# A causal transformer block with routed low-rank experts: its PSUM banks divided anew, and its side work dealt out one piece a step

## What is computed

```python
h = layernorm(x) * (1 + ca) + sa
q, k, v = split(h @ W_qkv.T + b_qkv)            # 16 heads of 16
o = softmax(causal(q @ k.T / 4)) @ v
x = x + ga * (o @ W_out.T + b_out)
h = layernorm(x) * (1 + cb) + sb
h1 = relu(mole(h; W1, b1, A1, B1, R1))          # 256 -> 1024
x = x + gb * mole(h1; W2, b2, A2, B2, R2)       # 1024 -> 256
# mole(x) = x @ W + b + (1/8) * sum_e softmax(x @ R)_e * (x @ A_e) @ B_e,   3 experts of rank 8
```

## Time and profile before

| | |
|---|---|
| median of 3 runs | 1724.15 us (1717.27 to 1735.03) |
| the profiled execution: its time, its span | 1730.61 us, 1728.9 us |
| busy: PE, PEld | 1412.8 us (82%), 796.4 us (46%) |
| busy: DVE, ACT, POOL | 961.8 us (56%), 685.5 us (40%), 561.6 us (32%) |
| mean granted clock of TensorE | 0.808 |

### The profile page before, as it was taken

How to read it: one execution, slowest core, us unless ns; L and a number is a source line. 1 busy time by engine, 2 the same in 40 slices (tenths; PEclk the granted TensorE clock), 3 DMA queues, 4 the chain that set the end, 5 groups by cost and what they waited for, 6 DMA issues and landing times. The chain is left out here.

```text
span 1728.9 us, 26273 instructions
## 1 busy us (share of the span) xinstructions
PE 1412.8 (82%) x10096; PEld 796.4 (46%) x10096; DVE 961.8 (56%) x1878; ACT 685.5 (40%) x935; POOL 561.6 (32%) x680
## 2 busy tenths in 40 slices
PE   4458898897998989899857988889888889899445
PEld 4334454544544434454423554536453445454245
DVE  6146566566576676763336556665756667761212
ACT  1113354353443445355522433344533444546210
POOL 5460151324440124332302341234432233233262
PEclk8666588788996888888965786888995899899758
DMA  5242223121321121220241223113121112100000
GB/s 149 77 133 79 74 81 101 34 64 31 99 71 49 38 55 57 67 77 20 80 114 47 75 87 83 34 37 104 51 75 40 48 30 71 50 10 13 31 18 13
DMA packets 83638, 106.68 MB, mean 62 GB/s; under 512 B 9002, under 2 KB 57074, under 8 KB 83516
## 3 DMA queue, kind: packets, MB, share of 16 engines
q1 hardware_dynamic: 83516, 105.01, 21.5%
HBM read 66.71 MB, written 37.75 MB: 60 GB/s over the span
## 5 line engine op out<-in xcount | busy, mean ns | idle before, releaser
L853 DVE TENSOR_REDUCE mx<-ps 128x1 f32<-128x512 f32 (+3 forms) x1152 | 706.8, 655 | 436.7 <-PE ps L570 241.0
L759 ACT ACTIVATE prob<-ps 128x1024 f32<-128x1024 f32 (+3 forms) x640 | 567.1, 896 | 700.1 <-PE ps L548 368.6
L570 PE MATMUL ps<-kst,qst 48*128 48x512 f32 (+3 forms) x1280 | 321.7, 497 | 135.5 <-DVE mx L853 108.5
L607 PE MATMUL ps<-prob,vw 128*17 128x512 f32 (+3 forms) x2560 | 353.3, 630 | 1.6 <-ACT o_sb L766 0.9
L543 PE MATMUL ps<-qst,kst 50*128 50x512 f32 (+3 forms) x1280 | 333.4, 519 | 8.3 <-ACT prob L759 5.6
L543 PEld LDWEIGHTS ps<-qst,kst 50*128 50x128 f32 x1280 | 138.7, 213 | 331.7 <-issue 146.2
L570 PEld LDWEIGHTS ps<-kst,qst 48*128 48x128 f32 x1280 | 155.2, 226 | 213.6 <-issue 158.4
L1030 POOL CAST hid_hi<-hidf 128x512 fp32r<-128x512 f32 x64 | 39.1, 612 | 341.7 <-ACT hidf L810 341.6
L578 PE MATMUL ps<-mask_q,pick 64*128 64x128 bf16 x1024 | 88.6, 255 | 0.0
L707 PE MATMUL ps<-w_hi,hid_hi 128*128 128x284 f32 x256 | 81.5, 339 | 8.2 <-POOL hid_lo L1031 8.1
L607 PEld LDWEIGHTS ps<-prob,vw 128*17 128x17 f32 x2560 | 44.3, 99 | 88.8 <-issue 62.9
(11 more groups left out here) (147 smaller groups left out, 1801.5 us busy)
## 6 DMA issues: line engine op xcount, KB each, us to landing
kst<-k_rows SPq DMA_DIRECT2D x160, 192.0 KB, 4.0
qst<-q_rows SPq DMA_DIRECT2D x64, 192.0 KB, 3.9
q_rows<-s_hi SPq DMA_DIRECT2D x64, 128.0 KB
k_rows<-s_hi SPq DMA_DIRECT2D x64, 128.0 KB
o_rows<-o_sb SPq DMA_DIRECT2D x32, 256.0 KB, 2.0
sx<-in_x SPq DMA_DIRECT2D x16, 256.0 KB, 2.9
q_rows<-sf SPq DMA_DIRECT2D x32, 128.0 KB
k_rows<-sf SPq DMA_DIRECT2D x32, 128.0 KB
```

The lines of the kernel that those rows point to most:

```text
L570: last = pe.matmul(ps[:, M_BANK + banks[a], at:at + width], qst[half, u % Q_BUFS, p, i * P:(i + 1) * P], kst[half, K_SLOT[u, c], p, 0:widt ...
L607: last = pe.matmul(ps[32 * h:32 * h + HD + 1, O_BANK, skip:BLK], vw[:, (NJ * b + t // 4) % V_BUFS, t % 4, g * GH + h, :], prob[:, s % P_BU ...
L759: act.activation(prob[:, s % P_BUFS, 2 * p:2 * p + 2, 0:width], ps[:, bank:bank + 2, 0:width], ACT.Exp).then_inc(a_free, 1)
L853: dve.tensor_reduce(mx[:, u % 2, a, both, i, c], ps[:, M_BANK + bank, 0:n * width].rearrange("p (h x) -> p h x", h=n), AX, ALU.max).then_i ...
```

## The change

PSUM is divided anew: three single banks for logits, three for maxima and turned maxima alone, one (`J_BANK`) for all pieces of jobs, one for the outputs. Logits still come in pairs, each taking the next two of the three banks; ACT now exponentiates 512 columns at a time, and a pair waits until the first half of the pair before it has been taken. `place()` works out the step of each piece: never two PE pieces in a step, a down projection as two pieces in two steps. A piece is emptied in the step after it: by ACT between its two pairs of exponentials, by DVE between the two halves of the maxima.

The denominators of a chunk of 512 tokens are loaded as 128x64 (`d_load`), inverted by DVE (`d_inv`), stored to `r_rows` (`d_store`), and the F jobs load the inverses broadcast; DVE's 128x512 reciprocal in `f_norm` is gone. POOL's standardising and splitting goes to DVE for S jobs 0 to 3 and in part for F jobs 14 and 15; W1 and W2 are split by ACT and DVE in step -20. `sx` has two buffers, `fx` three; S stores go out by halves (queries, then keys).

```diff
-A_SLOTS, M_BANK, M_BANKS, O_BANK = 2, 4, 3, 7
+A_BANKS, M_BANK, M_BANKS, J_BANK, O_BANK = 3, 3, 3, 6, 7
-S_START = [-24, -20, -15, -10, 14, 22, 58, 66, 112, 126, 146, 153, 174, 182, 214, 228]
-F_START = [24, 39, 56, 74, 104, 122, 168, 186, 204, 222, 240, 258, 276, 294, 328, 339]
+S_START = [-30, -26, -22, -18, 12, 20, 56, 64, 110, 120, 144, 152, 172, 180, 212, 226]
+F_START = [25, 38, 57, 73, 105, 121, 169, 184, 200, 215, 230, 246, 264, 280, 327, 328]
+D_START = [FIRST[NH // GH * (c + 1)] + 3 for c in range(NCHUNK)]
+S_CHAIN = [("s_load", 0), ("s_stat", 1), ("s_turn", 1), ("s_qk0", 2), ("s_qk1", 1), ("s_v", 1), ("s_store", 2)]
+D_CHAIN = [("d_load", 0), ("d_inv", 2), ("d_store", 1)]
+F_CHAIN = [("f_load", 0), ("f_norm", 2), ("f_proj", 3), ("f_stat", 2), ("f_turn", 2), ("f_route", 3), ("f_exp", 2),
+           ("f_gate", 1), ("f_zturn", 1), ("f_hid0", 2), ("f_hid1", 1), ("f_hid2", 1), ("f_hid3", 1),
+           ("f_down0", 3), ("f_down1", 1), ("f_exp2", 2), ("f_gate2", 1), ("f_zturn2", 1), ("f_low", 2),
+           ("f_out", 2)]
+EARLY, LATE = 4, NBLK - 2
+SPLIT_STEP = -20
+def place():
...
+            for piece, gap in chain:
+                s += gap
...
+                width = WIDTH.get(piece, 0)
+                while any(s + d in taken for d in range(width)):
+                    s += 1
...
+                def d_load(c):
+                    sp.wait_ge(o_stored, 16 * NH // GH * (c + 1))
...
+                    sp.dma_start(den[:], o_rows[c, :, HD, :].rearrange("h (k x) -> h k x", k=P // NH)
+                                 ).then_inc(d_in, 16)
+                def d_store(c):
+                    sp.wait_ge(d_done, c + 1)
+                    sp.dma_start(r_rows[c].rearrange("h (k x) -> (h k) x", k=P // NH), den[:]).then_inc(d_stored, 16)
                 def f_load(n):
-                    sp.wait_ge(o_stored, 16 * 4 * (c + 1))
+                    sp.wait_ge(d_stored, 16 * (c + 1))
...
-                        for g in range(2):
-                            sp.dma_start(fd[64 * g:64 * g + 64, k, :], o_rows[c, 2 * k + g, :, HD:HD + 1, cols]
-                                         .broadcast_to((GH, HD, TB))).then_inc(fo_in, 16)
+                        sp.dma_start(fd[:, k, :], r_rows[c, 8 * k:8 * k + 8, cols].unsqueeze(1)
+                                     .broadcast_to((8, HD, TB))).then_inc(fo_in, 16)
...
                 def logits(s, p):
-                    event = A_AT["exp", s, p]
-                    bank = event % A_SLOTS * 2
+                    event = GH * s + 2 * p
+                    banks = [(event + a) % A_BANKS for a in range(2)]
-                    if event >= A_SLOTS:
-                        pe.wait_ge(a_free, event - A_SLOTS + 1)
+                    if event >= A_BANKS - 1:
+                        pe.wait_ge(a_free, event + 2 - A_BANKS)
...
+                def job_bank(piece, n):
+                    if J_AT[piece, n]:
+                        pe.wait_ge(j_free, J_AT[piece, n])
...
-                def exponential(s, p):
+                def exponential(s, h):
...
-                    act.activation(prob[:, s % P_BUFS, 2 * p:2 * p + 2, 0:width], ps[:, bank:bank + 2, 0:width],
+                    if h % 2 == 0:
+                        act.wait_ge(a_full, 2 * s + h // 2 + 1)
+                    act.activation(prob[:, s % P_BUFS, h, 0:width], ps[:, event % A_BANKS, 0:width],
                                    ACT.Exp).then_inc(a_free, 1)
...
                     if 0 <= s < NSTEP:
                         exponential(s, 0)
                         exponential(s, 1)
+                    for piece, n in JOBS[s - 1]:
+                        if piece in drains:
+                            drains[piece](n)
+                    if 0 <= s < NSTEP:
+                        exponential(s, 2)
+                        exponential(s, 3)
...
-                def f_norm(n):
-                    dve.wait_ge(fo_in, 16 * 3 * KC * (n + 1))
-                    dve.reciprocal(fd[:], fd[:]).then_inc(rec_done, 1)
+                def d_inv(c):
+                    dve.wait_ge(d_in, 16 * (c + 1))
+                    dve.reciprocal(den[:], den[:]).then_inc(d_done, 1)
...
-                    for u, k in first + second:
+                    for u, k in first:
                         maximum(u, k)
+                    for piece, n in JOBS[s - 1]:
+                        if piece in drains:
+                            drains[piece](n)
+                    for u, k in second:
+                        maximum(u, k)
```

More of the change, by code:

```diff
@@ L71, in job_steps @@
+WHEN = place()
+BEGIN, END = min(S_START) - 1, max(WHEN.values()) + 3
+def job_steps():
+    at = {s: [] for s in range(BEGIN - 1, END + 1)}
+    for (piece, n), s in WHEN.items():
+        if WIDTH.get(piece, 0) == 2:
+            at[s].append((piece + "a", n))
+            at[s + 1].append((piece + "b", n))
+        else:
+            at[s].append((piece, n))
     return at
 JOBS = job_steps()
+J_ORDER = sorted((s, piece, n) for (piece, n), s in WHEN.items() if piece in WIDTH)
+J_AT = {(piece, n): k for k, (_, piece, n) in enumerate(J_ORDER)}
@@ L91, in pair_steps @@
 def pair_steps():
-    at = {s: [] for s in range(BEGIN - 5, END)}
+    at = {s: [] for s in range(BEGIN - 1, END)}
     for u in range(NU):
@@ L132, in rings @@
             take(("max", u, k, 1))
[L133 to L146, removed]
+    return at
+M_AT = maxima_banks()
 def key_loads():
     blocks = [(u, c) for u, (_, J, _) in enumerate(UNITS) for c in range(J + 1)]
-    at = {s: [] for s in range(BEGIN - 5, END)}
+    at = {s: [] for s in range(BEGIN - 1, END)}
     for kb, (u, c) in enumerate(blocks):
@@ L160, in key_loads @@
         b, J, _ = UNITS[u]
-        assert S_START[2 * (NJ * b + c) + 1] + S_PIECES["s_store"] < step < need, (kb, u, c, step, need)
+        assert WHEN["s_store", 2 * (NJ * b + c) + 1] < step < need, (kb, u, c, step, need)
         at[step].append(kb)
@@ L177, in query_loads @@
         b, J, _ = UNITS[u]
-        assert S_START[2 * (NJ * b + J) + 1] + S_PIECES["s_store"] < step < need, (u, step, need)
+        assert WHEN["s_store", 2 * (NJ * b + J) + 1] < step < need, (u, step, need)
         at[step].append(u)
@@ L436, in batch, with standardise, two_parts @@
             return n * TB // S
+        def standardise(eng, link, dst, src, mv, tmp, ready):
+            for t in range(TT):
+                last = eng.tensor_scalar(dst[:, t], src[:, t], mv[:, t, 0:1], tmp[:, 1, t:t + 1],
+                                         ALU.subtract, ALU.mult)
+                if t < TT - 1:
+                    link(last, wait=False)
+            last.then_inc(ready, 1)
+        def two_parts(eng, link, parts, src, ready):
+            link(eng.tensor_copy(parts[0], src))
+            eng.tensor_tensor(parts[1], src, parts[0].bitcast(F32), ALU.subtract).then_inc(ready, 1)
         with nc.Block() as block:
@@ L547, in logits @@
                             half = slice(64 * a, 64 * a + 64)
-                            last = pe.matmul(ps[:, bank + a, 0:P], pick[half, w - a + 1], mask_k[half, w - a + 1],
+                            last = pe.matmul(ps[:, banks[a], 0:P], pick[half, w - a + 1], mask_k[half, w - a + 1],
                                              start=False, stop=(w == 1))
@@ L1102, in f_low @@
                     pool.wait_ge(y_top, 2 * (n + 1))
[L1103 to L1107 removed]
+                    pool.tensor_tensor(fx[:, n % FX_BUFS], fx[:, n % FX_BUFS], yg[:], ALU.add).then_inc(y_done, 1)
```

472 lines of the change are left out of this document (244 added, 228 removed).

## The result

The changed kernel takes **1656.06 us** (median of 4 runs, 1652.96 to 1660.92) against 1728.22 for the kernel before in the same comparison: a ratio of 0.9591, 95% interval 0.9529 to 0.9653. That is faster, inside the range of 1515 to 1715, but 72 us instead of the 117 forecast. The profiled execution took 1658.97 us, its span 1657.2.

The account below looks back on a forecast made before the run. The steps, 1492.8 us, bound the kernel: 1080 us of work, 226 of clock, 187 of waiting. Steps -109, preparation -13 and tail +5 us took 1728.9 to 1612, a median of 1607, range 1515 to 1715.

Parts of the forecast that it names:

- Idle of PE: In the steps, the sum of PE's idle terms: -28 - 20 - 10 - 8 + 24 + 10 = -32 us.
- Reciprocals: In the steps, 14 long reciprocals leave DVE at 2 us each: 28 us less PE idle (8 to 35).
- Draining later: In the steps, DVE joins the maxima before emptying a piece: 10 us less PE idle (0 to 20).
- S turns: In the steps, twelve S turns wait about 2 us each for POOL's rows: 24 us more idle (0 to 40).
- Logits: In the steps, pairs in three banks wait for one exponential: 10 us more idle over 81 bare steps (0 to 49).
- -38 us of clock: In the steps, clock regained with the -32 us of idle, at 1.2 us per us of idle.
- For pieces dealt evenly I take another 30 us of clock: In the steps, bare runs become shorter: 30 us of clock gained (0 to 100) besides that from idle.
- Preparation: Before step 0: earlier queries, DVE's splitting and moved weights' split against one job bank, -13 us (-30 to +5).
- Tail: After the steps: inverses' extra trips and one shared bank against DVE in place of POOL, +5 us (-10 to +15).
- The steady clock: Rival for the steps: with nearly every step filled, PE stops falling to 1.2 GHz; 1509 us, chance 0.20.
- DVE still sets the pace: Rival for the steps: maxima waits return, S turns cost 40 us, the clock gains nothing; 1700 us, chance 0.16.
- The three banks: Rival for the steps: PE stops for exponentials and the clock falls more often, under 0.78; 1755 us, slower, chance 0.14.

Follow-up runs that it names:

- experiment 3: Changed kernel with DVE's 128x512 reciprocals back for all 16 token blocks, in place of the four 128x64 inversions: 1712.58 us, ratio 0.9919.
- experiment 5: Changed kernel with a piece's bank emptied at the end of the piece's own step again, not a step later: 1685.93 us, ratio 0.9781.
- experiment 1: Changed kernel with load and statistics of token blocks 4 to 15 one step earlier, so S turns stand two steps behind the statistics: 1606.65 us, ratio 0.932.
- experiment 4: Changed kernel with two banks for logits in place of three, the third left unused: 1719.29 us, ratio 0.9969.
- experiment 6: Changed kernel with POOL standardising and splitting for all S and F jobs again: 1676.04 us, ratio 0.9732.
- experiment 11: Kernel with S turns later, four S jobs earlier and bare steps filled (1584.26 us), with weights' split and gates' bounds moved later before step 0: 1582.94 us.
- experiment 10: Changed kernel with S turns a step later and four unread matmuls of 512 columns in each of 81 steps without a piece: 1603.49 us, ratio 0.927.
- experiment 8: Changed kernel with S turns a step later and two unread matmuls of 512 columns in each of 81 steps without a piece: 1593.61 us, ratio 0.9248.

## Why the prediction was right, and where its size was off

Undone one by one, the reciprocals are worth 57 us, draining later 30, and DVE in POOL's place 20; the S turns' waits cost 49. That adds up to 58 of the 72 us, an estimate, since parts need not add. The rest is left for the queries' wait, fewer bare steps and the banks, which no run parted.

**Idle of PE, right: -30 us against -32.** Its terms, one by one. Reciprocals: 28.9 against 28 (experiment 3). Draining later: 10.0 of wait against 10, though only 5.8 of idle (experiment 5). The queries' wait: 15.6 gone, 8 taken. S turns: 35.9 instead of 5.8, so 30 against 24; the 4.7 us of POOL and the step's end were rightly read, the wait is 3.0 us rather than 2. Logits: 25 us more against 10, inside its 0 to 49; the mean of 0.095 us a step keeps the sign that was given. Of the 47 us that the maxima's wait lost, experiment 3 gives 21 to the reciprocals; 26 are left for fewer bare steps, where 20 stood, and for the maxima's own banks, which no run parted. The joined maxima lost 24 us: 10.0 by draining later, 6.5 by the reciprocals (12.6 in experiment 3 against 6.1), and 8 are left. The one bank of the pieces was put at nothing in the steps, since a step's attention lies between two pieces. PE does wait there, 23.6 us in all, but the shared banks of the kernel before cost some 20 us in the same way, so that the difference is small.

**Clock, the step that failed: "-38 us of clock" and "For pieces dealt evenly I take another 30 us of clock".** PE's busy time fell by 33.6 us in all. 57 matmuls fewer lie in the steps, at a mean of 1272/9470 = 0.13 us some 8 us, close to the 9 taken for moved pieces; 26 us are left for the clock, not 68. The rate of 1.2 us of clock per us of idle was not far off: 26 us for 30 of idle is 0.9, and between the changed kernel and experiments 1, 3 and 4, idle moved by -25.0, +28.9 and +36.9 us, and busy time by -33, +29 and +19, a rate of 0.5 to 1.3. (Experiment 5, with +5.8 and +30, fits no such rate.) That accounts for some 10 of the missing 42 us. What does not show anywhere is the term of the even dealing. With the long reciprocals back, all the rest of the change (239 steps with one piece instead of 159, with the rest bare or holding two or three) leaves idle at 186 and the steps at 0.83, as before.

Nor do the S turns' waits hide that gain. The prediction priced them at 24 us of idle and 1.2 times as much of clock, 53 us in all, and taking them out gave 49.4 us (1656.06 to 1606.65). Without them, in experiment 1, idle is 55 us under that of the kernel before and busy time 67 us, some 60 of it clock once the moved pieces are taken off: 1.1 us for each us of idle, and again no 30 us beside it. Executions of the same steps differ by 17 us of busy time, but all three kernels lack the term. So what the runs show in place of the term is nothing beyond the idle itself. No run undid the dealing alone, and why 39 bare steps fewer bring no more is open. That experiment 1 lands on the forecast's 1607 is chance: it takes out waits that the forecast had counted in, and the clock that it counted on did not come.

**Preparation: -6.4 against -13.** The changed kernel's profile has the latest start of step 0 of the nine with this preparation; over all nine, against the one execution of the kernel before, it is -6.4 to -11, so a part of the miss may lie in this execution. The stores' wait fell as argued: ACT waited 39.3 us in all for key and query rows before and 12.3 after (9.2 for key rows, 3.1 for query rows). DVE in place of POOL gives 5.9 to 10.5 (experiment 6), where 2.2 us for three jobs, 6.6, was taken. PE's busy time ahead of step 0 rose from 43.3 to 49.1 us for as many matmuls (253 and 251), its clock fell from 0.62 to 0.56, and the prediction had no term for that; in the nine executions this clock lies anywhere from 0.54 to 0.70. What was sized too small is the one bank. PE's waits before step 0 that are new (us in total, times, longest):

```profile
PE ps L668 <- ACT sf L836: 9.4, 8, 1.5
PE ps L679 <- DVE vw L975: 8.8, 3, 5.5
```

They make 18 us where 9 were taken. The longest comes from DVE's order of work (timeline of DVE, then PE):

```profile
60.91 5.78 DVE L949 TENSOR_TENSOR w_lo<-prob,w_hi 128x2048 fp32r<-128x2048 f32 x2
66.62 0.68 DVE L975 TENSOR_TENSOR vw<-ps,bv_sb 128x512 f32<-128x512 f32 x1
...
67.44 1.08 PE L679 MATMUL ps<-ident,sx 128*128 128x128 f32 x4 [5.52 <-DVE vw L975]
```

The drain of the values stands behind 5.78 us of weights' split, and PE's turn behind the drain. Experiment 11 moved the split and the gates' bounds together, and step 0 came 2 to 6.5 us sooner; how much is due to either is open. The Trainium skill, "Perfetto Trace Analysis", section "Matmuls", wants independent groups of matmuls in different banks. The trace agrees here, where no step's attention lies between two pieces: 18 us of waits for drains of the one bank.

**Tail: -1.7 against +5.** DVE in place of POOL is worth 6.5 to 11.6 us there (experiment 6), not 4. That is enough to make up the difference, but executions of the same tail differ by 5 us, and no run parted the other terms.

**The rivals.** The steady clock did not come; even at 0.93 (experiment 10) PE's added work stood in its place. That DVE still sets the pace was half right: its wait is still the largest, and S turns wait 35.9 us, near the 40 that this case named, but the clock did gain. The three banks cost 25 us of idle, and the steps' clock stayed at 0.85, over the 0.78 from which they would have decided.

**Open:** how much of the clock is due to the length and order of waits rather than to their sum. Draining in the same step had 81 us more at half speed for 6 us more idle, with short waits exchanged for longer ones; the S turns' waits of 3 us went with 1.3 us of clock for each us, the 71 more short waits of two logit banks with 0.5. That points to length, but the two differ by no more than executions of the same steps do (17 us of busy time), and no run changes the length alone.

## What to carry to other kernels

Price a wait that stops PE with the clock that it costs: taking the twelve waits of 3 us out gave 25 us of idle and 49 us of time. Do not count a gain of clock for evenness on top of the idle that it removes, unless a run shows it. A plan that deals work evenly has to keep the distance between a slow helper's start and PE's use of its result, counted in steps of the shortest length. Where one bank serves several engines' drains, look at what each drain stands behind on its own engine. Before reading a few tens of us of clock or a few us of a stretch as an effect, compare two executions of the same work. And before buying clock with idle-time work, see that it takes the place of a wait: beyond that it costs what it brings.

## What the runs showed of the hardware

- Work added to PE need not cost time: 144 matmuls in the S turns' waits took 103 us at half speed out of the steps around them, and the time did not rise (1649.32 against 1656.06 us, not separated).
- A higher clock is not yet less time: from experiment 8 to 10 the steps' clock rose from 0.90 to 0.93, and their length changed by 1.0 us (one execution each).
- Six runs of one kernel (experiment 11) range over 1.9%, in the order of their mean clock from 0.900 to 0.868 with no exception.
